# One constant product between every two heads of the first maxima, and batch 1's projections some heads later

## The chip, the cores and the metric

The kernel runs on one core of one Trainium2 chip, as one launch. The metric is the device time of one execution in microseconds. Before the change it was 619.75 us, the median of three runs (617.78 to 620.05). One execution was taken by the hardware profiler: 615.73 us, of which 614.0 us are the span of its trace. Five engines work at once and meet through semaphores: PE (TensorE, matmuls), DVE (VectorE), ACT (ScalarE), POOL (GpSimd) and SP (SyncE, which here only starts DMAs). TensorE is granted one of two clocks, 1.2 or 2.4 GHz, which the profile writes as 0.50 and 1.00.

## The reference

Two layers work on x of 16 batches x 256 rows x 128 columns. The first is attention with 16 heads of 8 columns each, the second a transformer block with a mixture of 8 experts. The change lies in the first. Cut to what matters:

```
x = x + layernorm(attn(layernorm(x)))           # layer 1
    qkv = x @ w_qkv.T + b_qkv                    # 16 heads of 8 columns
    a   = softmax(q @ k.T / sqrt(128))           # per batch and head: 256 x 256
    out = (a @ v) @ w_o.T + b_o + x
x = x + layernorm(ffn(layernorm(x)))            # layer 2
    y = layernorm(x + mha(x));  z = layernorm(y + moe(y))   # argmax over 8 experts
```

All of it is float32.

## The kernel before

Layer 1 computes the scores of every head twice. The first time (line 203, `scores_for_max`) the queries stand on the partitions, so that DVE can take each query's maximum over the keys straight from PSUM (line 357, `maxima`). The maxima are turned by DVE and written by SP's DMAs into a further row of the tile `q`. The second time (line 220, `scores`) the keys stand on the partitions, the maximum is subtracted as that further row, ACT takes the exponential (line 529), and PE multiplies with the values (line 234, `attend`).

A head has only 8 columns, and its operands lie in one of four strips of 32 partitions, `32 * (h % 4)`. A head's first scores use 24 of the array's 128 rows (or 8, for heads 12 to 15, whose keys are in `kraw`), its second scores 26 or 27. A head is two matmuls of 128 x 256 in float32, one for each half of the rows; the trace has two records for each of these, so four records for a head. The heads are issued in the order n = 0 to 15 with h = n ^ 2, so that consecutive heads lie in different strips.

PE's work is an order written out by hand. After the start (weights turned, batch 0 normalised and projected, seven constant products), a first stage makes the sixteen maxima of batch 0 and has nothing else of that batch to do. Batch 1's preparation is put between its heads: `prep_x(1)` turns the normalised x on PE (line 170), `prep_qk` makes queries and keys (line 177) and `prep_v` the values (line 185). Then come the iterations i = 0 to 16. Each has eight groups g, and in group g stand two heads of the first scores of batch i+1 and two heads of the second scores of batch i, now and then an attend (g = 3, 5, 7, and 1 for the last quarter of batch i-1), and the preparation of batch i+2.

PE waits in `scores_for_max` until DVE has read the PSUM bank of three heads before (`a_free`), and in `prep_x(1)` until POOL has normalised batch 1 (`xn_ok`, line 644). `keep_warm(n)` (line 161) is n matmuls of constant bfloat16 tiles, 128 x 128 by 128 x 512, into `psO`; nobody reads the result. The names in rows: `km` and `kraw` are keys, `qp` and `q` queries, `psA` the bank of the first scores, `psB` of the second, `psO` of the attends, `misc` of the preparation, `warm` the constant tile.

Layer 2 works on x when layer 1 has ended, at about 313 us.

Of the kernel before, what the change touches and what calls it, by code (L numbers as in the profile page):

```python
# [34 lines left out]
def first_layer(nc, x, w_qkv, b_qkv, w_o, b_o, ident, identh, minus_half, xs, out, kept, loads2, loaded2, w, loads,  # L35
                loaded):

    with ExitStack() as ctx:
# [66 lines left out]
        def fits(i, d):  # L105

            return 0 <= i + d <= LAST
# [46 lines left out]
        def _(pe):  # L154
            T = nc.tensor

            def begin(*name):

                pe.wait_ge(S["free"], turns[name])

            def keep_warm(n):

                for _ in range(n):
                    T.matmul(psO[:, :], warm[:, 0:P], warm[:, :], start=True, stop=True)

            def prep_x(b):
                begin("xT", b)
                pe.wait_ge(S["xn_ok"], b + 1)
                for c in range(2):
                    last = T.transpose(misc[:, c * P:(c + 1) * P], xn[:, b % 2, c, :], ident[:, :])  # L170
                last.then_inc(S["full"], 1)

            def prep_qk(b, k, t):
                if t == 0:
                    pe.wait_ge(S["free"], turns[("xT", b)] + 1)
                    begin("qk"[k], b)
                made = T.matmul(misc[:, t * L1:(t + 1) * L1], wqk[:, k, t, :], xnT[:, b % 2, :], start=True,  # L177
                                stop=True)
                if t == 1:
                    made.then_inc(S["full"], 1)  # L180
# [8 lines left out]
            def prep_v(b):  # L189
                begin("v", b)  # L190
                token_major(xnT[:, b % 2, :], 0)

            def scores_for_max(b, n):

                h = n ^ 2
                if n == 0:
                    pe.wait_ge(S["q_ok"], 4 * b + 4)
                    pe.wait_ge(S["k_ok"], 2 * b + 2)
                    pe.wait_ge(S["km_ok"], b + 1)
                pe.wait_ge(S["a_free"], count(16 * b + n - 2))  # L200
                depth = 24 if h < 12 else C1
                for c in range(2):
                    last = T.matmul(psA[:, (16 * b + n) % 3, c * L1:(c + 1) * L1],  # L203
                                    query_part(b, h, depth, c),
                                    keys(b, h, depth, slice(0, L1)), start=True, stop=True)
                last.then_inc(S["a_full"], 1)

            def scores(b, h):

                if h % HALF == 0:  # L210
                    pe.wait_ge(S[f"mrow{h // HALF}"], 16 * HALF * (b + 1))
                if b < LAST or h < 3:
                    pe.wait_ge(S["b_free"], count(16 * b + h - 2))
                elif h < 5:
                    pe.wait_ge(S["a_free"], 16 * B1)
                else:
                    pe.wait_ge(S["b_free"], 16 * b + h - 4)
                depth = 26 if h < HALF else 27
                for c in range(2):
                    last = T.matmul(bank_of(b, h)[:, c * L1:(c + 1) * L1],  # L220
                                    keys(b, h, depth, slice(c * P, (c + 1) * P)), queries(b, h, depth, slice(0, L1)),
                                    start=True, stop=True)
                last.then_inc(S["b_full"], 1)

            def attend(b, quad):

                pe.wait_ge(S["b_free"], 16 * b + 4 * quad + 4)
                if quad == 0:
                    pe.wait_ge(S["v_ok"], b + 1)
                if quad % 2 == 0:  # L230
                    pe.wait_ge(S["o_ev"], 2 * b + quad // 2)
                for c in range(2):
                    for j in range(4):
                        last = T.matmul(psO[32 * j:32 * j + 32, (quad % 2) * L1:(quad % 2 + 1) * L1],  # L234
                                        v32[:, b % SLOTS, c, 4 * quad + j, :], pr[:, (4 * quad + j) % PRING, c, :],
                                        start=(c == 0), stop=(c == 1))
                last.then_inc(S["av_done"], 1)

            def project(b):
                pe.wait_ge(S["onT_ok"], b + 1)  # L240
                begin("out", b)
                token_major(onT, 1)

            def iteration(i):
                here, next_, done = fits(i, 0), fits(i, 1), fits(i, -1)
                for g in range(8):
                    if next_:
                        scores_for_max(i + 1, 2 * g)
                        scores_for_max(i + 1, 2 * g + 1)
                    if here and next_:  # L250
                        scores(i, 2 * g)
                        scores(i, 2 * g + 1)
                    if here and not next_ and g % 2 == 0:
                        for h in range(2 * g, 2 * g + 4):
                            scores(i, h)
                    if here and g in (3, 5, 7):
                        attend(i, g // 2 - 1)
                    if g == 0 and i >= 2 and here:
                        prep_v(i)
                    if g == 1 and done:  # L260
                        attend(i - 1, 3)
                    if g == 1 and fits(i, 2):
                        prep_x(i + 2)
                    if g in (2, 4) and fits(i, 2):
                        prep_qk(i + 2, g // 2 - 1, 0)
                        prep_qk(i + 2, g // 2 - 1, 1)
                    if g == 6 and done:
                        project(i - 1)
# [35 lines left out]
            keep_warm(7)  # L304
            for n in range(16):
                scores_for_max(0, n)
                if n == 1:
                    prep_x(1)
                if n in (3, 5):
                    prep_qk(1, n // 2 - 1, 0)  # L310
                    prep_qk(1, n // 2 - 1, 1)
                if n == 7:
                    prep_v(1)
                if n in (9, 11, 13):
                    keep_warm(2)
            pe.wait_ge(S["v_ok"], 1)
            for i in range(LAST + 2):
                iteration(i)
# [1449 lines left out]
```

## Time and profile before

| | |
|---|---|
| runs, median (lowest to highest) | 619.75 us (617.78 to 620.05) |
| profiled execution | 615.73 us |
| its span | 614.0 us |
| mean granted clock of TensorE | 0.891 |
| PE busy, whole span | 522.8 us, 85% |
| DVE busy | 451.0 us, 73% |
| ACT busy | 359.4 us, 59% |
| POOL busy | 312.6 us, 51% |

The shares are over two layers with different limits, so they don't say what one stage waits for. The stage of the change runs from 12.55 us (head 0 of the first maxima) to 38.1 us, and iteration 0 from there to about 59.3 us. A matmul's time in the trace contains its way through the array, so the time that one step costs PE is read from start to start.

### The profile page before, as it was taken

To read this page: it belongs to the slowest core of one execution; us is meant where nothing else is said; L and a number is where in the kernel's file an instruction comes from. 1 tells how busy PE (TensorE), PEld (TensorE's weight loads), DVE (VectorE), ACT (ScalarE), POOL (GpSimd) and SP (SyncE) were. 2 spreads that over 40 slices of the span, in tenths; PEclk is the share of its full clock that TensorE was granted. 3 is DMA by queue.
4 is the path that set the end of the run, shared out by engine and by line. 5 is a ranking of instruction groups with operands and counts; after the bars stand their busy time and mean duration, and the time that the engine had idled before them with its cause. 6 is when DMAs were issued, how large, how long until landed. Compare 5 with 4: busy or idle time off the path is not lost. (4 is left out here: it accounts for less than half of the span.)

```text
span 614.0 us, 15928 instructions
## 1 busy us (share of the span) xinstructions
PE 522.8 (85%) x5194; PEld 375.8 (61%) x5194; DVE 451.0 (73%) x1278; ACT 359.4 (59%) x976; POOL 312.6 (51%) x522
## 2 busy tenths in 40 slices
PE   7999999999999999999954799988866269999910
PEld 4556666666666656666633577766645269999910
DVE  4346788888888879888833789999586626788860
ACT  3216667666776755676641798877643035776660
POOL 5402233344455546622234548878884600467776
PEclk9558999999999989999995999999856569999975
DMA  6001423111001110101120000000010222244233
GB/s 188 1 1 28 149 70 56 24 24 20 6 18 20 19 21 19 19 5 19 20 53 17 36 2 2 1 4 11 21 39 34 88 55 64 33 65 61 28 35 30
DMA packets 36036, 21.62 MB, mean 35 GB/s; under 512 B 11242, under 2 KB 34291, under 8 KB 35956
## 3 DMA queue, kind: packets, MB, share of 16 engines
q1 hardware_dynamic: 18450, 10.65, 7.5%
q0 software_dynamic: 6640, 4.92, 5.7%
q10 hardware_dynamic: 10866, 5.03, 3.1%
q8 instruction: 43, 0.70, 0.5%
q14 instruction: 37, 0.30, 0.2%
HBM read 10.11 MB, written 8.12 MB: 30 GB/s over the span
## 5 line engine op out<-in xcount | busy, mean ns | idle before, releaser
L357 DVE TENSOR_REDUCE nmax<-psA 128x2 f32<-128x512 f32 x256 | 164.8, 686 | 55.8 <-PE psA L203 55.1
L529 ACT ACTIVATE pr<-psB 128x512 f32<-128x512 f32 x250 | 136.0, 595 | 97.7 <-PE psB L220 96.4
L203 PE MATMUL psA<-km,qp 24*128 24x256 f32 x768 | 127.4, 426 | 1.4 <-DVE nmax L357 1.4
L220 PE MATMUL psB<-q,km 26*128 26x256 f32 (+1 forms) x752 | 112.0, 414 | 0.2 <-DMA q<-mT 0.2
L203 PEld LDWEIGHTS psA<-km,qp 24*128 24x128 f32 x768 | 79.5, 197 | 35.0 <-DVE nmax L357 24.0
L1689 POOL DMA_INDIRECT out<-wz,ys x39 | 63.3, 1624 | 53.3 <-ACT wz L1644 44.4
L657 POOL TENSOR_TENSOR km<-kraw,rows_of 128x768 f32<-128x768 f32 x15 | 22.0, 1467 | 113.4 <-ACT kraw L503 113.4
L220 PEld LDWEIGHTS psB<-q,km 26*128 26x128 f32 (+1 forms) x752 | 69.8, 191 | 1.4 <-DMA q<-mT 1.1
L234 PE MATMUL psO<-pr,v 128*32 128x256 f32 x1024 | 69.5, 389 | 0.1
L1241 ACT ACTIVATE prob<-psS,nbias 128x128 f32<-128x128 f32 x128 | 45.5, 384 | 8.6 <-DVE nbias L1059 8.5
L234 PEld LDWEIGHTS psO<-pr,v 128*32 128x32 f32 x1024 | 27.0, 110 | 33.1 <-issue 21.6
L1545 DVE TENSOR_TENSOR hT<-psH,e_nb1T 128x512 f32<-128x512 f32 x39 | 27.0, 692 | 25.8 <-PE psH L1506 17.8
L1506 PE MATMUL psH<-yT,own 128*128 128x128 f32 x312 | 42.7, 281 | 0.0
L203 PE MATMUL psA<-kraw,qp 8*128 8x256 f32 x256 | 41.3, 416 | 0.0
L1520 PE MATMUL psO<-e_w,hT 128*128 x312 | 41.2, 275 | 0.0
L1357 POOL DMA_INDIRECT y_sorted<-y_all,slot_i x32 | 32.4, 1012 | 16.9 <-DVE slot_i L1108 9.0
L1506 PEld LDWEIGHTS psH<-yT,own 128*128 128x128 f32 x312 | 39.5, 199 | 0.0
L1627 ACT ACTIVATE own<-e_w 128x512 f32 x39 | 24.3, 623 | 23.6 <-PEq L813 18.1
L1520 PEld LDWEIGHTS psO<-e_w,hT 128*128 128x128 f32 x312 | 38.0, 192 | 0.0
L177 PE MATMUL misc<-xnT,wqk 128*128 128x256 f32 x120 | 36.4, 429 | 0.2
L220 PE MATMUL psB<-q,kraw 27*128 27x256 f32 x248 | 36.0, 400 | 0.0
L630 POOL TENSOR_SCALAR ve<-mv_r 128x2 f32<-128x2 f32 x16 | 3.8, 236 | 61.3 <-DVE mv_r L331 61.3
(227 smaller groups left out, 1136.2 us busy)
## 6 DMA issues: line engine op xcount, KB each, us to landing
q<-mT SPq DMA_DIRECT2D x256, 1.0 KB
ys<-y_sorted SPq DMA_DIRECT2D x39, 72.0 KB, 1.9
e_w<-W ACTq DMA_DIRECT2D x1, 2048.0 KB
e_w<-W ACTq DMA_DIRECT2D x4, 512.0 KB
xs<-x_all SPq DMA_DIRECT2D x16, 128.0 KB
out<-x_all SPq DMA_DIRECT2D x15, 128.0 KB, 3.7
x_all<-x SPq DMA_DIRECT2D x1, 1536.0 KB, 10.3
out<-wz,ys POOLq DMA_INDIRECT x39, 3.3
```

The costliest lines, as they stand in the source:

```text
L177: made = T.matmul(misc[:, t * L1:(t + 1) * L1], wqk[:, k, t, :], xnT[:, b % 2, :], start=True, stop=True)
L203: last = T.matmul(psA[:, (16 * b + n) % 3, c * L1:(c + 1) * L1], query_part(b, h, depth, c), keys(b, h, depth, slice(0, L1)), start=True, ...
L220: last = T.matmul(bank_of(b, h)[:, c * L1:(c + 1) * L1], keys(b, h, depth, slice(c * P, (c + 1) * P)), queries(b, h, depth, slice(0, L1)), ...
L234: last = T.matmul(psO[32 * j:32 * j + 32, (quad % 2) * L1:(quad % 2 + 1) * L1], v32[:, b % SLOTS, c, 4 * quad + j, :], pr[:, (4 * quad + j ...
L357: V.tensor_reduce(nmax[:, b % 2, hf, :, at], psA[:, (16 * b + n) % 3, :].rearrange("p (c m) -> p c m", c=2), AX.X, ALU.max, negate=True).t ...
L529: A.activation(pr[:, h % PRING, :, :].rearrange("p c l -> p (c l)"), bank_of(b, h), ACT.Exp, scale=SCALE1).then_inc(S["b_free"], 1)
L1241: A.activation(prob[:, n, c, h, :], psS[s][:, u * P:(u + 1) * P], ACT.Exp, bias=nbias[:, s, u:u + 1], scale=SCALE2, accum_out=den[:, n, c, ...
L1357: G.indirect_dma_start(y_sorted, bass.IndirectOffsetOnAxis(slot_i[:, j:j + 1], 0), y_all[:, j, :], None).then_inc(sent, 16)
L1506: last = T.matmul(psH[t % 2][:, f * P:(f + 1) * P], own[:, t % 3, f * P:(f + 1) * P], yT[:, t % 3, :], start=True, stop=True)
L1520: last = T.matmul(to, hT[:, t % 2, f, :], w["w2"][:, f, bass.ds(e, P)], start=False, stop=(f == NF - 1))
L1545: V.tensor_tensor(hT[:, t % 2, :, :], psH[t % 2][:, :].rearrange("p (f n) -> p f n", f=NF), w["nb1T"][:, bass.ds(e, NF)].unsqueeze(2).broa ...
L1689: G.indirect_dma_start(out, bass.IndirectOffsetOnAxis(ids[:, t % RING, P:P + 1], 0), wz[:, t % WRING, :], None, compute_op=ALU.add).then_i ...
```

## The change

Before, the constant products of the first stage came in three groups of two, after n = 9, 11 and 13, and batch 1's preparation after n = 1 (x), 3 and 5 (queries, keys) and 7 (values). Heads 0 and 1, 2 and 3 and so on stood side by side.

After, the preparation comes after n = 4, 6, 8 and 10, three constant products after n = 2, and one after each of the eleven other heads. Iteration 0 gets two constant products in each of its groups 0 and 1. In all there are fourteen constant products in the first stage in place of six, and four in iteration 0 in place of none. The computation is the same.

```diff
@@ iteration(i) of PE
                     if here and g in (3, 5, 7):
                         attend(i, g // 2 - 1)
+                    if i == 0 and g in (0, 1):
+                        keep_warm(2)
                     if g == 0 and i >= 2 and here:
                         prep_v(i)
@@ the first stage of PE
             keep_warm(7)
             for n in range(16):
                 scores_for_max(0, n)
-                if n == 1:
+                if n == 2:
+                    keep_warm(3)
+                elif n == 4:
                     prep_x(1)
-                if n in (3, 5):
-                    prep_qk(1, n // 2 - 1, 0)
-                    prep_qk(1, n // 2 - 1, 1)
-                if n == 7:
+                elif n in (6, 8):
+                    prep_qk(1, n // 2 - 3, 0)
+                    prep_qk(1, n // 2 - 3, 1)
+                elif n == 10:
                     prep_v(1)
-                if n in (9, 11, 13):
-                    keep_warm(2)
+                else:
+                    keep_warm(1)
             pe.wait_ge(S["v_ok"], 1)
             for i in range(LAST + 2):
                 iteration(i)
```

The first place is PE's stream at the start of the first maxima. A row is a matmul as issued; `x4` of line 203 is two heads side by side, `x2` is one head. Before:

```order
L164 MATMUL psO<-warm 128x512 x7
L203 MATMUL psA<-km,qp 128x256 x4
L170 MATMUL misc<-ident,xn 128x128 x2
L203 MATMUL psA<-km,qp 128x256 x4
L177 MATMUL misc<-xnT,wqk 128x256 x2
L203 MATMUL psA<-km,qp 128x256 x4
L177 MATMUL misc<-xnT,wqk 128x256 x2
```

The same place after the change:

```order
L164 MATMUL psO<-warm 128x512 x7
L203 MATMUL psA<-km,qp 128x256 x2
L164 MATMUL psO<-warm 128x512
L203 MATMUL psA<-km,qp 128x256 x2
L164 MATMUL psO<-warm 128x512
L203 MATMUL psA<-km,qp 128x256 x2
L164 MATMUL psO<-warm 128x512 x3
L203 MATMUL psA<-km,qp 128x256 x2
L164 MATMUL psO<-warm 128x512
L203 MATMUL psA<-km,qp 128x256 x2
L170 MATMUL misc<-ident,xn 128x128 x2
```

No two heads stand side by side any more, here or in the rest of the stage: there is a constant product or a piece of preparation between any two.

The second place is PE's stream from the last heads of the stage into iteration 0, where a group of the iteration is a row of line 203 and one of line 220. Before:

```order
L203 MATMUL psA<-kraw,qp 128x256 x4
L203 MATMUL psA<-km,qp 128x256 x4
L220 MATMUL psB<-q,km 128x256 x4
L203 MATMUL psA<-km,qp 128x256 x4
L220 MATMUL psB<-q,km 128x256 x4
L170 MATMUL misc<-ident,xn 128x128 x2
```

The same place after the change:

```order
L203 MATMUL psA<-kraw,qp 128x256 x2
L164 MATMUL psO<-warm 128x512
L203 MATMUL psA<-km,qp 128x256 x4
L220 MATMUL psB<-q,km 128x256 x4
L164 MATMUL psO<-warm 128x512 x2
L203 MATMUL psA<-km,qp 128x256 x4
L220 MATMUL psB<-q,km 128x256 x4
L164 MATMUL psO<-warm 128x512 x2
L170 MATMUL misc<-ident,xn 128x128 x2
```

The groups of iteration 0 keep their heads side by side; two constant products come behind each of the first two. The other engines' streams have the same instructions in the same order as before.

## Rows read from the trace of the kernel before

**Rows 1.** The page's 40 slices: PE busy and granted clock in tenths.

```profile
PE   7999999999999999999954799988866269999910
PEclk9558999999999989999995999999856569999975
```

**Rows 2.** Stretches: length, busy us (instructions) of PE, PEld, DVE, ACT, POOL, clock, DMA.

```profile
10.00:16.00 6.00, 4.43 (x29) 2.73 (x29) 4.51 (x15) 2.13 (x6) 2.91 (x7) 1.00 0.56 154
16.20:22.00 5.80, 5.80 (x20) 3.42 (x17) 2.08 (x4) 0.84 (x2) 0.29 (x1) 0.50 0.01 3
...
28.00:35.20 7.20, 7.20 (x24) 2.79 (x22) 3.42 (x6) 0.00 (x0) 3.78 (x9) 0.50 0.01 1
...
43.00:50.20 7.20, 7.20 (x47) 4.29 (x50) 2.62 (x8) 2.39 (x5) 0.00 (x0) 0.50 0.02 3
50.40:59.30 8.90, 8.90 (x116) 5.50 (x108) 6.94 (x14) 6.83 (x16) 4.24 (x7) 1.00 0.01 3
60.00:200.00 140.00, 139.46 (x1704) 88.42 (x1696) 119.76 (x273) 96.06 (x202) 59.34 (x101) 1.00 0.19 45
```

**Rows 3.** Who waited for whom from 60 to 300 us: total, times, longest.

```profile
DVE nmax L357 <- PE psA L203: 32.9, 71, 2.0
```

**Rows 4.** PE in order of time around the fall: start, us, operation, records, idle before.

```profile
10.95 1.67 PE L164 MATMUL psO<-warm 128*128 128x512 bf16 x7
12.55 1.14 PE L203 MATMUL psA<-km,qp 24*128 24x256 f32 x8
15.26 0.41 PE L170 MATMUL misc<-ident,xn 128*128 128x128 f32 x2 [1.57 <-POOL xn L644]
15.60 1.57 PE L203 MATMUL psA<-km,qp 24*128 24x256 f32 x8
```

**Rows 5.** PE in order of time: a pair and two constant products, later a lone head.

```profile
26.29 2.08 PE L203 MATMUL psA<-km,qp 24*128 24x256 f32 x8
28.31 1.03 PE L164 MATMUL psO<-warm 128*128 128x512 bf16 x2
29.27 2.08 PE L203 MATMUL psA<-km,qp 24*128 24x256 f32 x8
...
35.80 0.76 PE L203 MATMUL psA<-km,qp 24*128 24x256 f32 x1
...
36.35 0.63 PE L203 MATMUL psA<-km,qp 24*128 24x256 f32 x1
...
36.78 1.05 PE L203 MATMUL psA<-km,qp 24*128 24x256 f32 x2
```

**Rows 6.** PE in order of time in iteration 10, a head alone at full clock.

```profile
214.16 1.13 PE L203 MATMUL psA<-km,qp 24*128 24x256 f32 x4
215.67 0.48 PE L203 MATMUL psA<-km,qp 24*128 24x256 f32 x1 [0.39 <-DVE nmax L357]
...
216.85 0.71 PE L185 MATMUL misc<-wvo,xnT 128*128 128x128 f32 x4
```

**Rows 7.** Stretches around the same place, columns as in Rows 2.

```profile
210.00:217.40 7.40, 7.01 (x78) 4.66 (x72) 7.15 (x12) 4.09 (x9) 6.96 (x9) 1.00 0.02 3
217.60:220.90 3.30, 3.30 (x32) 1.90 (x32) 2.33 (x8) 1.76 (x4) 2.38 (x6) 0.50 0.02 4
```

**Rows 8.** PE in order of time in iteration 0: first group, rise of the clock, end.

```profile
38.09 0.79 PE L203 MATMUL psA<-km,qp 24*128 24x256 f32 x1 [0.25 <-DVE nmax L357]
...
49.69 1.35 PE L234 MATMUL psO<-pr,v 128*32 128x256 f32 x16
50.97 0.49 PE L203 MATMUL psA<-km,qp 24*128 24x256 f32 x2
...
52.06 1.13 PE L177 MATMUL misc<-xnT,wqk 128*128 128x256 f32 x4
...
59.22 0.49 PE L203 MATMUL psA<-km,qp 24*128 24x256 f32 x2
```

**Rows 9.** The page's costliest group: DVE's maxima.

```profile
L357 DVE TENSOR_REDUCE nmax<-psA 128x2 f32<-128x512 f32 x256 | 164.8, 686 | 55.8 <-PE psA L203 55.1
```

## The prediction

> **What bounds the kernel now.** I read the 40 slices first. PE is busy nine tenths or more nearly everywhere in the first half, and in slices 1 and 2 its clock is at 0.5 although PE is full [rows 1]. So the stretches of time come next. From 16.2 to 50.2 us the granted clock is 0.50, the lower of the two levels, and PE is busy without a gap: 7.20 of 7.20 us in two of the stretches [rows 2]. From 50.4 us on it is 1.00, and stays so over the 140 us that follow. The waits show that DVE waits for PE's scores 71 times between 60 and 300 us, 32.9 us in all [rows 3]: in layer 1 PE is what the others wait for, and time that PE loses or wins early in the layer arrives at its end. Layer 2's work on x can't start before that, so it arrives at the end of the kernel too.
>
> The order of time shows what the clock did at its fall. PE worked through seven constant products and two heads, then waited 1.57 us for POOL's normalised x, turned it, and was in the middle of the next two heads when the clock fell at about 16.2 us [rows 4]. It rose at about 50.3 us, while the first attend of iteration 0 was running, with a projection and the two heads of each kind shortly before it [rows 8]. What the change can win is therefore the wait (1.57 us) and a part of the 34 us at the lower clock. What it costs is read from start to start of PE's steps.
>
> **What a step costs.** At the lower clock two heads side by side take 26.29 to 28.31, 2.02 us, for eight records [rows 5]. The two heads lie in different strips of the array and run at the same time. A lone head is seen in the same stage: its four records start at 35.80, 36.35 and (two) from 36.78 on, with a busy time of 1.05 from 36.78, so it ends at 37.83, 2.03 us after its start; at first the pair before it still ran in other strips, its last records ran alone [rows 5]. A head alone costs what two heads cost. At the full clock the same holds: eight records 1.14 us [rows 4], four records of a lone head 1.13 us [rows 6]; from start to start a full-clock block is 50.97 to 52.06, 1.09 us [rows 8]. I take 1.07, and 2.02/1.07 = 1.89 as the ratio between the two clocks.
>
> The page "TensorE: Matmul & The Clock Gate" of the Trainium skill says in "Part 3: Packing small matmuls" that matmuls in different row strips run concurrently and that matmuls stay in order. It speaks against this change: a full-height product between two heads takes the partner away from each. The trace has the same thing with its own numbers, above.
>
> Seven constant products take 10.95 to 12.55, 1.60 us, or 0.23 each at the full clock [rows 4], so 0.43 each at the lower one by the ratio. Two of them there take 28.31 to 29.27, 0.96 us, change of operation included [rows 5]. A single one between two heads isn't in the trace at either clock. Its bounds are 0.43 (no more than its stream) and 0.96 (as much as two); I take 0.96 - 0.43 = 0.53, since the pair's row is the nearest.
>
> **The sum, on the path of the clock as it was.** All of it lies on PE, which is the engine waited for.
> - Lost pairs: eight blocks of two heads become sixteen of one. 8 x 2.02 = +16.2 us.
> - Constant products of the first stage: before 3 x 0.96 = 2.9; after eleven single ones, 5.8, and one group of three, 0.96 + 0.43 = 1.4, so 7.2. +4.3 us (bounds: +3.2 to +9.1).
> - Iteration 0: two groups of two, +1.9 us (+1.0 if the clock is full there). Its heads stay side by side.
> - The wait: -1.6 us. Batch 1's x was ready at 15.2 us, and `prep_x(1)` now comes after five heads, so it waits for nothing. Queries, keys and values of batch 1 come later by some heads, but are wanted only in iteration 0 and after it. DVE needs 0.69 us for a head's maxima [rows 9] against 2.5 us of PE, so it waits more and delays nobody; the PSUM bank is always free.
> - The full-clock time before the fall, from 12.55 to 16.2, is now full of work. The 1.57 us that were a wait do work that would cost 1.57 x 1.89 = 2.97 later: -1.4 us beyond the wait itself.
>
> This gives +19.4 us. Moved preparation costs the same wherever it stands.
>
> **The clock's own path.** Two terms are left. The fall can come somewhat later than 16.2, since the gap before it is filled. What the trace shows for lone heads at the full clock is iteration 10: a lone head for 1.13 us, 0.39 us of waiting, three heads at once, a small projection, and then the clock is at 0.50 for 3.3 us, where PE had been busy 7.01 of the 7.40 us before [rows 6, 7]. The new stage is a row of such lone heads with products between. And from 28.0 to 35.2 three blocks of two heads alternated with three groups of two products, 100% busy, and the clock stayed at 0.50 [rows 2]; the new stage has fewer products per microsecond (0.53 in 2.55 us of a step, before 0.96 in 2.98). So it should fall early and not rise again inside the stage. I allow 0 to 6 us more at full clock and take 2; each is worth 0.89: -1.8 us. The rise in iteration 0 came 12.2 us after the iteration began at 38.1 [rows 8]. With four products in its first groups it can come earlier, 0 to 9 us; I take 5, each worth 1 - 1/1.89 = 0.47: -2.4 us.
>
> 19.4 - 1.8 - 2.4 = +15.2 us. The profiled execution was 615.7 (614.0 of span, 1.7 around it), 4.0 below the median of the runs; on the profile's own footing I expect 630.9, and against the median of 619.75 it is 635. Bounds of this case: with 6 and 9 us both at their best +9.9, with both at zero +19.4, and with the single product at 0.43 or 0.70 another -1 or +2. Own range 628 to 641.
>
> **Rivals.**
> - The clock holds. "Part 1: The HAM clock gate" of the page named above, in the Trainium skill, ties the clock to how busy PE has been, and a reader of that alone would expect a filled PE to keep it; the trace disagrees by the 34 us of full PE at 0.50 [rows 2]. As a mechanism here: the only gap in front of the fall goes, and PE stays at 1.00 from 12.55 on. The old stage at full clock would be 2.1 (the old full part without the wait) + 21.65/1.89 = 13.6 us; the eight lost pairs add 8 x 1.07 = 8.6, eight more products 8 x 0.23 = 1.8: 24.0 against 25.5. Iteration 0 turns 12.1 us into 6.4 and adds 0.9: -4.8. In all -6.3: 613.5. Since a microsecond at the lower clock costs 0.47, this rival decides up to some 13 us at the lower clock between 12.55 us and the old rise; with more the kernel is slower. Against it stands iteration 10 [rows 6, 7].
> - A return in the middle: the clock falls early, and the two projections with full array after n = 6 and 8 bring it back at about n = 8. Before, the first of them stood in the stretch from 16.2 to 22.0 us with two heads on each side, and the clock stayed at 0.50 [rows 2]. By the ratio: about 14.2 of 24.0 full-clock us lie before that point, 3.65 of them run full, so (14.2 - 3.65) x 0.89 = 9.4 us are lost: 24.0 + 9.4 = 33.4 against 25.5, +7.9, and iteration 0 gives -4.8. +3.1: 623.
> - The pairs are not lost: a head overlaps with something else in the array, and only products and wait count: 4.3 + 1.9 - 1.6 - 1.4 - 2.4 = +0.8: 620.5. Against it stand both lone heads [rows 5, 6]; constant products never overlapped with the heads beside them.
> - It falls and iteration 0 stays at the lower clock until its end at 59.2 [rows 8]: +19.4 and (59.2 - 50.3) x 0.89 = 7.9, 647. The attend that stood before the old rise is still there, so this is unlikely.
>
> **Chances.** The forecast 0.74; the clock holds 0.09; a return in the middle 0.08; pairs not lost 0.05; low through iteration 0 0.04. A difference under 0.5%, 3 us, can't be told from no change. Faster by more than that is the first rival, 0.09. The third rival and the margin of the second give 0.04 for no change. The rest, 0.87, is slower. The range reaches from the return in the middle to the top of the forecast's own: 622 to 641.
>
> **What the profile after would show.** The rows of line 164 with one product at a time between `x4` rows of line 203, each head some 2.0 us from its start to the product; clock 0.50 from somewhere in 16 to 22 us to about 60; the start of iteration 0 (the first row of line 220) at about 53 instead of 38; the wait of line 170 gone; L357's waits for PE longer in the first stage. After iteration 0 the same picture as before, some 15 us later. I would be wrong if the clock is at 1.00 in the stage, or if a head followed by a product takes less than 1.8 us at the lower clock.

## The result, and the profile after

The changed kernel took 632.09 us in the median of four runs (624.35 to 637.01) against 619.75 us (617.78 to 620.05). The ratio is 1.0226, with a 95% interval from 1.0154 to 1.0297 (the two medians alone give 1.020): slower, as forecast (635, 622 to 641). That it is slower is clear of the noise; whether by more than 2% is not. The profiled execution is the quickest of the four, 624.35 us with a span of 622.6, so 8.6 us above the profiled one of before.

The page of the kernel after: PE's busy share and the granted clock in 40 slices of 15.6 us, and DVE's maxima with their idle time. The answers to [rows 1] and [rows 9].

```profile
PE   8999999999999999999963899999857259999910
PEclk9658899999999999999995999797766569999975
...
L361 DVE TENSOR_REDUCE nmax<-psA 128x2 f32<-128x512 f32 x256 | 165.5, 686 | 62.1 <-PE psA L203 61.3
```

The clock holds into slice 1 and is low in slice 2 and the beginning of slice 3. DVE's maxima (L361 here is line 357 of the kernel before) cost the same and wait 6 us longer for PE. The stretches of the same kernel, columns as in [rows 2]:

```profile
12.30:21.50 9.20, 8.95 (x35) 5.20 (x36) 5.01 (x12) 0.39 (x2) 3.40 (x7) 1.00 0.13 31
21.70:49.30 27.60, 27.13 (x56) 14.55 (x56) 7.38 (x15) 2.78 (x7) 7.20 (x14) 0.50 0.00 1
49.40:52.20 2.80, 2.47 (x18) 1.39 (x18) 1.17 (x4) 0.54 (x2) 0.00 (x0) 0.50 0.01 4
52.40:65.80 13.40, 13.38 (x157) 8.71 (x156) 9.97 (x22) 9.23 (x20) 3.66 (x7) 1.00 0.02 3
66.10:69.30 3.20, 3.20 (x32) 1.89 (x25) 1.11 (x3) 0.98 (x2) 0.29 (x1) 0.50 0.58 154
```

The clock is 1.00 to 21.6 us, 0.50 to 52.3, and once more 0.50 from 66.0 to 69.4. PE in order of time, the answer to [rows 4, 5 and 8]: start, busy us, operation, records, idle before.

```profile
12.26 1.13 PE L203 MATMUL psA<-km,qp 24*128 24x256 f32 x4
13.64 1.13 PE L203 MATMUL psA<-km,qp 24*128 24x256 f32 x4 [0.25 <-issue]
14.69 0.39 PE L164 MATMUL psO<-warm 128*128 128x512 bf16 x1
15.01 1.13 PE L203 MATMUL psA<-km,qp 24*128 24x256 f32 x4
...
19.26 0.44 PE L170 MATMUL misc<-ident,xn 128*128 128x128 f32 x2
...
24.45 2.07 PE L203 MATMUL psA<-km,qp 24*128 24x256 f32 x4
26.45 0.61 PE L164 MATMUL psO<-warm 128*128 128x512 bf16 x1
26.98 2.07 PE L203 MATMUL psA<-km,qp 24*128 24x256 f32 x4
...
49.38 0.80 PE L203 MATMUL psA<-km,qp 24*128 24x256 f32 x2
...
65.86 1.44 PE L234 MATMUL psO<-pr,v 128*32 128x256 f32 x12
```

Each row of line 203 is now one head (`x4`, before `x8` for two), and one head takes 24.45 to 26.45, 2.00 us, at the lower clock. A product between two heads takes 26.45 to 26.98, 0.53 us. (The record of one product at 13.3 us is missing from the trace; its time is there as "issue".) The wait in front of line 170 is gone. Who waited from 12 to 50 us:

```profile
DVE nmax L361 <- PE psA L203: 24.5, 16, 3.3
```

Each of the sixteen maxima waits for PE, which is full. Before, from 12 to 38.1 us, these waits came to 13.9 us.

| from start to start | before | after | |
|---|---|---|---|
| first maxima (first head to iteration 0) | 12.55 to 38.09: 25.5 us | 12.26 to 49.38: 37.1 us | +11.6 |
| iteration 0 to its last attend | 38.09 to 58.22: 20.1 us | 49.38 to 65.86: 16.5 us | -3.6 |
| the rest | to 614.0 | to 622.6 | +1.0 |

(The stage began 0.3 us earlier in the profile after, which makes up the total of 8.6, but for rounding.)

The boundary at 38.09 is not a clean one. The rows from 35.80 on in [rows 5] are no head of the stage: they are the first head of iteration 0, which began beside the stage's last pair. Of that pair these rows are the beginning:

```profile
35.23 0.80 PE L203 MATMUL psA<-kraw,qp 8*128 8x256 f32 x2
35.82 1.07 PE L203 MATMUL psA<-kraw,qp 8*128 8x256 f32 x4
```

By the price of a pair it ended at about 37.25 (35.23 + 2.02, an estimate); the second head of iteration 0 waited for DVE and started at 38.09. So some 0.84 us of the 25.5 belong to iteration 0. In the profile after, both first heads of iteration 0 start at 49.38, and there is no such piece.

### The profile page after: what moved, and what is told of

It reads as the page before. It is cut to its first block and busy times, and to the rows that moved or that the text cites. A ratio compares the mean times of both kernels' runs of the same rounds, so it can differ in the third digit from the quotient of the medians.

```text
span 622.6 us, 15949 instructions
## 1 busy us (share of the span) xinstructions
PE 534.8 (86%) x5203; PEld 383.9 (62%) x5206; DVE 449.5 (72%) x1278; ACT 358.7 (58%) x976; POOL 314.1 (50%) x522
## 5 line engine op out<-in xcount | busy, mean ns | idle before, releaser
L361 DVE TENSOR_REDUCE nmax<-psA 128x2 f32<-128x512 f32 x256 | 165.5, 686 | 62.1 <-PE psA L203 61.3
L203 PE MATMUL psA<-km,qp 24*128 24x256 f32 x768 | 130.2, 413 | 1.9 <-DVE nmax L361 1.1
L220 PE MATMUL psB<-q,km 26*128 26x256 f32 (+1 forms) x752 | 108.4, 405 | 0.0
L203 PEld LDWEIGHTS psA<-km,qp 24*128 24x128 f32 x768 | 80.9, 190 | 37.0 <-DVE nmax L361 22.2
L220 PEld LDWEIGHTS psB<-q,km 26*128 26x128 f32 (+1 forms) x752 | 67.5, 187 | 0.5 <-DMA q<-mT 0.4
L203 PE MATMUL psA<-kraw,qp 8*128 8x256 f32 x256 | 45.5, 417 | 0.0
L1361 POOL DMA_INDIRECT y_sorted<-y_all,slot_i x32 | 32.6, 1019 | 16.9 <-DVE slot_i L1112 9.0
L1631 ACT ACTIVATE own<-e_w 128x512 f32 x39 | 24.3, 624 | 23.8 <-PEq L817 18.2
L203 PEld LDWEIGHTS psA<-kraw,qp 8*128 8x128 f32 x256 | 29.2, 192 | 10.8 <-DVE nmax L361 6.5
L177 PE MATMUL misc<-xnT,wqk 128*128 128x256 f32 x120 | 35.4, 420 | 0.3
```

Source lines behind the costliest of these rows:

```text
L220: last = T.matmul(bank_of(b, h)[:, c * L1:(c + 1) * L1], keys(b, h, depth, slice(c * P, (c + 1) * P)), queries(b, h, depth, slice(0, L1)), ...
L361: V.tensor_reduce(nmax[:, b % 2, hf, :, at], psA[:, (16 * b + n) % 3, :].rearrange("p (c m) -> p c m", c=2), AX.X, ALU.max, negate=True).t ...
L1361: G.indirect_dma_start(y_sorted, bass.IndirectOffsetOnAxis(slot_i[:, j:j + 1], 0), y_all[:, j, :], None).then_inc(sent, 16)
```

## The experiments

Theory L: the loss is the pairs. A full-height product or a piece of preparation between any two heads makes sixteen blocks of eight. Rival P: the loss is the twelve more constant products. Rival C: the moved preparation lets the clock fall. Each ratio below is to the kernel before on the same chip, whose median was 619.78 us beside e1 to e4 and 617.88 beside e5 to e8; it stands with its 95% interval and differs from the quotient of the medians by up to 0.4%. The changed kernel did not run beside them, so where a run is compared with its 632.09 us the ratios are the better guide. All stages named in the text are read in the one profiled execution of each kernel. The line numbers in rows move by up to four with each edit: L207 and L181 of e2_strip are L203 and L177 before, and L356 of e5_late_prep is L357.

**Heads in pairs again (e1_pairs).** All fourteen products of the changed kernel and its preparation, one head later still, behind odd heads alone (`...` stands for calls of the preparation, here and below):

```diff
-                if n == 2:
-                    keep_warm(3)
-                elif n == 4:
+                if n == 5:
                     prep_x(1)
-                elif n in (6, 8):
+                if n in (7, 9):
                     ...
-                elif n == 10:
+                if n == 11:
                     prep_v(1)
-                else:
-                    keep_warm(1)
+                keep_warm({1: 2, 3: 4, 5: 1, 7: 1, 9: 1, 11: 1, 13: 2, 15: 2}.get(n, 0))
```

> The changed kernel with its heads in pairs again: all fourteen constant products and the same late preparation, but only behind a head of odd number, so that two heads stand side by side (products after n = 1, 3, 5, 7, 9, 11, 13, 15: 2, 4, 1, 1, 1, 1, 2, 2). Theory L (the lost pairs are the price): eight blocks fewer, 8 x 2.0 = 16 us at the lower clock, so 616 or less; since work is then packed closer the clock may also hold, and the first maxima then end near 28 us and not 49: 605 to 612. Rival P (the twelve more constant products are the price): they are all still there, so 628 to 634. Rival C (the moved preparation lets the clock fall and that is the price): also 628 to 634.

Measured: 608.91 us, ratio 0.9818 (0.9749 to 0.9887). Same work as the changed kernel, and by the medians 23 us faster (the ratios are 0.9818 and 1.0226). Its stretches and first rows:

```profile
12.70:28.30 15.60, 15.60 (x91) 9.40 (x92) 11.03 (x25) 3.17 (x8) 7.17 (x14) 1.00 0.08 19
28.50:31.70 3.20, 3.20 (x19) 1.41 (x18) 1.66 (x5) 0.58 (x2) 2.86 (x8) 0.50 0.02 3
31.90:45.30 13.40, 13.38 (x157) 8.65 (x156) 9.98 (x22) 9.23 (x20) 3.87 (x8) 1.00 0.02 3
```

```profile
12.61 1.14 PE L203 MATMUL psA<-km,qp 24*128 24x256 f32 x8
13.69 0.60 PE L164 MATMUL psO<-warm 128*128 128x512 bf16 x2
```

The stage ends at 28.85 us, after 16.2 us, at full clock to its last pair. That is 20.9 us less than the changed stage, and not the pairs alone: the changed stage's work, put to the full clock, is 9.4 + 27.8/1.89 = 24.1 us, so the pairs are 7.9 of the 20.9 and the clock, which now holds, is 13.0. P and C have no place left as the main cost: the products and the late preparation are both there.

**Pairs lost without any product (e2_strip).** The kernel before, with heads that share a strip side by side in batch 0's first maxima:

```diff
+        def first_order(n):
+            return n // 8 * 8 + n % 8 // 2 + 4 * (n % 2)
-                h = n ^ 2
+                h = first_order(n) if b == 0 else n ^ 2
```

> The kernel before, with one difference: in batch 0's first maxima the heads come in the order 0 4 1 5 2 6 3 7 8 12 9 13 10 14 11 15, so that the two heads side by side share a strip of the array and cannot run at the same time. No product is added and nothing else moves. Theory L: a pair takes eight records one after the other, at the lower clock 8 x 0.43 + 0.3 = 3.7 us in place of 2.0, so 8 x 1.7 = +14 us: 630 to 636. Rivals P and C: nothing that they name is changed, so 618 to 621.

Measured: 630.83 us, ratio 1.0175 (1.0118 to 1.0232). Some 11 of the changed kernel's 12 us, with no product added. Two heads in PE's order of time, and the stretches:

```profile
15.34 3.77 PE L207 MATMUL psA<-km,qp 24*128 24x256 f32 x8
19.05 2.07 PE L181 MATMUL misc<-xnT,wqk 128*128 128x256 f32 x4
```

```profile
15.10:49.20 34.10, 34.10 (x80) 21.71 (x79) 9.80 (x18) 3.17 (x8) 8.19 (x16) 0.50 0.01 2
49.30:62.70 13.40, 13.40 (x88) 8.44 (x85) 6.87 (x15) 5.53 (x11) 0.00 (x0) 0.50 0.01 2
```

The two heads take 3.71 us, as worked out, against 2.02 side by side in different strips. The stage lasts from 12.15 to 49.2 us, 37 us, as long as the changed one. This run isolates the pairs, since its clock takes nearly the old course: it falls at 15.0 us (before 16.2) and rises 13.5 us into iteration 0 (before 12.2).

**The products of iteration 0 alone (e3_it0).**

```diff
+                    if i == 0 and g in (0, 1):
+                        keep_warm(2)
```

> The kernel before with only the change's four constant products in groups 0 and 1 of iteration 0. Cost 1.9 us at the lower clock; the rise of the clock may come earlier by up to 9 us, each worth 0.47. Theory L: between +2 and -2.5 us, 617 to 622. Rival P (a constant product costs far more than its stream, about 1 us each over the whole path): +4, 624.

Measured: 614.98 us, ratio 0.9944 (0.9879 to 1.0009), so the sign isn't certain; it is below the expected 617 to 622. The stretches of its trace:

```profile
15.40:38.20 22.80, 22.55 (x79) 12.46 (x79) 9.29 (x19) 3.10 (x8) 7.92 (x16) 0.50 0.01 1
38.40:45.90 7.50, 7.50 (x46) 4.34 (x50) 3.72 (x10) 2.55 (x5) 0.00 (x0) 0.50 0.01 2
46.10:56.80 10.70, 10.68 (x128) 6.74 (x120) 7.71 (x15) 7.49 (x16) 3.63 (x7) 1.00 0.02 4
```

The clock rises 7.8 us after the iteration's start in place of 12.2, and the time from that start to the last attend falls from 20.1 to 18.7 us. This part of the change costs nothing here and may give a little.

**The stage alone (e4_noit0).** The changed kernel without the two lines of e3_it0.

```diff
-                    if i == 0 and g in (0, 1):
-                        keep_warm(2)
```

> The changed kernel without its four constant products in iteration 0; the first stage is the changed one. Theory L: the stage holds the whole loss, so as slow as the changed kernel: 629 to 636, later rise of the clock in iteration 0 than 3 us after its start. Rival P: a third of the added products gone, so a third of the loss: 628.

Measured: 636.43 us (635.98 to 636.83), ratio 1.0276 (1.0226 to 1.0326), 0.4 us above the expected 629 to 636. Its stretches:

```profile
13.00:16.80 3.80, 3.80 (x15) 2.17 (x16) 2.17 (x7) 0.00 (x0) 3.37 (x7) 1.00 0.25 60
17.00:54.60 37.60, 37.60 (x78) 19.73 (x76) 10.05 (x19) 3.16 (x8) 7.21 (x14) 0.50 0.00 1
54.70:68.00 13.30, 13.30 (x86) 8.48 (x86) 6.46 (x15) 5.02 (x11) 0.00 (x0) 0.50 0.01 2
```

Here the clock fell at 16.9 us, although the stage is word for word that of the changed kernel, whose clock fell at 21.6. The stage lasts 12.90 to 54.62, 41.7 us against 37.1 there. Counted from each stage's own start, the full clock lasted 4.0 us here and 9.4 there: 5.4 us at 0.89 each are 4.8, where 4.6 was measured. So the moment of the fall differs between executions of the same instructions, and with it this stage is 11.6 or 16.2 us longer than before. The clock rose 13.5 us after the iteration's start, against 3 us with the products, and iteration 0 took 20.8 us to its last attend, against 16.5.

**The late preparation alone (e5_late_prep).**

```diff
-                if n == 1:
+                if n == 5:
                     prep_x(1)
-                if n in (3, 5):
+                if n in (7, 9):
                     ...
-                if n == 7:
+                if n == 11:
                     prep_v(1)
```

> The kernel before with only batch 1's preparation moved: x, queries, keys and values of batch 1 behind n = 5, 7, 9 and 11 in place of 1, 3, 5 and 7; the six constant products stay behind 9, 11 and 13, heads in pairs. The first wait of 1.6 us goes. Theory L: the move costs nothing, 616 to 620, with the clock falling near 16 us as before. Rival W (the wait is what lets the clock fall, so without it the clock holds through the stage): 603 to 608.

Measured: 610.85 us, ratio 0.9851 (0.9783 to 0.9918), between the two theories and better than L said. In its trace the wait for POOL is gone and the clock falls all the same:

```profile
12.34 1.15 PE L203 MATMUL psA<-km,qp 24*128 24x256 f32 x12
14.32 3.18 PE L203 MATMUL psA<-km,qp 24*128 24x256 f32 x12 [0.83 <-DVE nmax L356]
17.43 0.69 PE L170 MATMUL misc<-ident,xn 128*128 128x128 f32 x2
```

```profile
12.40:15.50 3.10, 2.27 (x20) 1.74 (x20) 2.73 (x9) 0.00 (x0) 2.63 (x6) 1.00 0.44 107
15.70:36.80 21.10, 20.63 (x70) 11.65 (x69) 8.57 (x18) 3.17 (x8) 7.77 (x15) 0.50 0.01 1
```

With nothing between the first six heads PE now waits 0.83 us for DVE instead. But this profiled execution is the slowest of the four (617.66; the others 608.4 to 612.6), so it doesn't show where the others gained. It refutes rival W only as a certainty: the wait for POOL is not needed for the fall. What the wait does in the other executions stays open. With the heads in pairs the late preparation is no cost: the whole interval lies below 1. Why the median is 7 us lower, when the wait was 1.6, isn't shown.

**Pairs, with products where the heads are thin (e6_dense), and the same with iteration 0's products (e8_dense_it0).** The preparation stands as in e5_late_prep, and thirteen products replace the six, eight of them behind the last three pairs, two of which have heads of 8 rows. e8_dense_it0 has the lines of e3_it0 besides.

```diff
+                keep_warm({1: 2, 3: 2, 5: 1, 11: 2, 13: 3, 15: 3}.get(n, 0))
```

> Heads in pairs, preparation behind n = 5, 7, 9, 11, and twelve... in all thirteen constant products, more of them where a pair has only 8 rows: behind n = 1, 3, 5, 11, 13, 15: 2, 2, 1, 2, 3, 3; none in iteration 0. Theory L with the clock: the stage runs at full clock to its end (in the run with pairs the clock fell at 28.4 us, behind the pairs of 8 rows), 602 to 608. Rival P (products cost more than they give): above the 609 of the run with pairs.

> The kernel of e6_dense with the change's four constant products in iteration 0 as well. If the clock is at 1.00 when iteration 0 begins, they cost 4 x 0.22 + 0.2 = 1.1 us and give nothing: 1 us above e6_dense. If it had fallen there, they bring it back earlier: up to 3 us below.

Measured: 604.31 us, ratio 0.9752 (0.9683 to 0.9821), and 603.74 us, ratio 0.9764 (0.9700 to 0.9827). The stretches of e6_dense:

```profile
12.30:28.00 15.70, 15.49 (x92) 9.29 (x95) 11.52 (x27) 3.16 (x9) 7.83 (x15) 1.00 0.11 28
28.10:43.20 15.10, 15.08 (x170) 10.18 (x168) 11.54 (x25) 10.02 (x21) 6.46 (x13) 1.00 0.02 4
43.30:200.00 156.70, 155.96 (x1905) 98.61 (x1906) 133.96 (x301) 107.78 (x226) 68.21 (x111) 1.00 0.19 42
```

From 12.3 to 200 us the lower clock doesn't come at all: stage 15.6 us (12.26 to 27.89), the maxima of DVE (16 x 0.69 = 11.0) now fairly close behind, iteration 0 15.3 us. Both kernels beat the one before by some 14 us and, by the medians, the changed one by some 28. The four products in iteration 0 make no difference that can be measured; what they were forecast to cost there, 1.1 us, is smaller than the intervals. In the trace of e8_dense_it0 iteration 0 takes 15.4 us, and PE waits 0.6 us in it for the DMA that writes the maxima into `q` (0.2 in e6_dense): with PE at full clock throughout, something else begins to hold it up.

**Lone heads kept at full clock (e7_lone_three).** The changed kernel's lone heads with three products behind each but n = 6 and 8, and none in iteration 0:

```diff
-                if n == 2:
-                    keep_warm(3)
-                elif n == 4:
+                if n == 4:
                     ...
-                else:
-                    keep_warm(1)
+                if n not in (6, 8):
+                    keep_warm(3)
```

> The changed kernel's lone heads and preparation, but three constant products behind each head but n = 6 and 8 (42 in all), none in iteration 0. It separates the two parts of the loss. Theory L: the clock holds at 1.00 and a lone head then costs 1.07 us, so 16 x 1.07 + 42 x 0.22 + preparation 3.0 + changes 1.2 = 30.6 us for the stage against 25.5, and iteration 0 gains 4 to 6: 617 to 623, faster than the changed kernel in spite of 28 more products. Rival: if lone heads let the clock fall whatever stands between, 42 products at 0.43 and sixteen blocks of 2.0 take some 60 us: 650.

Measured: 623.59 us (615.1 to 627.1), ratio 1.0114 (1.0032 to 1.0197): 0.6 us above the expected 617 to 623, and far from the rival's 650.

```profile
16.20:46.50 30.30, 29.82 (x118) 15.65 (x120) 12.66 (x27) 3.19 (x9) 10.60 (x21) 1.00 0.00 1
46.60:61.80 15.20, 15.20 (x170) 10.34 (x170) 11.10 (x24) 9.97 (x21) 3.63 (x7) 1.00 0.02 4
```

```profile
19.78 1.13 PE L203 MATMUL psA<-km,qp 24*128 24x256 f32 x4
20.84 0.82 PE L164 MATMUL psO<-warm 128*128 128x512 bf16 x3
21.59 1.13 PE L203 MATMUL psA<-km,qp 24*128 24x256 f32 x4
```

The stage lasts 16.16 to 46.53, 30.4 us, where 30.6 was worked out, at 1.00 throughout. With 28 products more in it the stage is 6.7 us shorter than the changed one, since it has the clock. The medians agree (623.59 against 632.09), though the two intervals of the ratio overlap a little; and the mean granted clock of all ten runs is 0.898 to 0.914, of the changed kernel's four 0.872 to 0.882.

It is 19 us slower than e6_dense. Of that the two traces show 14.7 us in the stage: eight lost pairs at 1.06 (8.5) and 29 more products at 0.22 (6.4) make 14.9. The profiled execution also began the stage 3.9 us later than that of e6_dense. No instruction before that point was changed, but eight of them, batch 0's projections of queries and keys, took 3.63 us where e6_dense has 1.96: the step of the lower clock (read from the rows; the windows give 1.00 there). So the price of the pairs is there at either clock, and nearly double at the lower (2.02 against 1.06).

## Why the prediction was right

**The lost pairs** were put at eight blocks of 2.02. A lone head took 2.00 us in the profile after, two heads in one strip 3.71 (e2_strip), which alone made the kernel before 11 us slower. Putting the pairs back (e1_pairs) turned 632.09 into 608.91, but there the clock changed as well. Shown, and the main term. The row from which the prediction read the price of a lone head was the first head of iteration 0 and not one of the stage; the price holds all the same.

**The single product**, not in the trace before and taken at 0.53 between 0.43 and 0.96, was 0.53.

**The wait** went, as said. **The moved preparation** cost nothing, as said (e5_late_prep); what it gained in the runs was not foreseen.

**The fall of the clock** was allowed 0 to 6 us later and taken at 2. From the stage's start on, the full clock lasted 3.63 us before, 9.36 in the profiled execution after and 3.99 in that of e4_noit0, with the same instructions: 5.73 and 0.36 later. Put into the sum, 16.2 + 4.3 - 1.6 - 1.4 = 17.5, and 17.5 - 5.73 x 0.89 = +12.4 us for the stage against +11.6 measured; with 0.36 it is +17.2 against +16.2. The step was right, the size is one that the executions spread over. The 0.8 and 1.0 us that are left over are about the size of a term that the prediction had at nothing: the 0.84 us by which 38.09 lies behind the stage's last pair. That piece is gone in the profile after, and the prediction took 38.1 for the plain start of iteration 0.

**The rise in iteration 0** was taken at 5 us earlier; it was 9.2 in the profile after and 4.4 in e3_it0. For the iteration that gives +1.0 (the four products counted at the full clock, since the time at the lower one is counted by itself) and -9.2 x 0.47 = -4.3, so -3.3, against -3.6; in e3_it0 +1.0 - 2.1 = -1.1, against -1.4. This term was undersized for the profiled execution.

**The total**, +15.2, is an execution with a fall at 18.2 us and a rise 7 us into the iteration. The profiled one had both better and is 8.6 us above, so 6.6 below the 630.9 that were expected on its footing, and iteration 0 began at 49.4 and not at about 53; the median of the runs is 12.3 above. That the median came so near to 15.2 rests on a choice inside a spread: 2 and 5 us were picked from 0 to 6 and 0 to 9. The runs carry their mean granted clock: 0.882 at 624.35 us and 0.872 at 633.01. The time at the lower clock is twice one minus that, by the span: 146.9 us of 622.6 and 161.6 us of 631.3, 14.7 us more, which at 0.47 cost 6.9 of the 8.7 between the two. At 631.17 us (0.875) it is 4.9 of 6.8, but at 637.01 (0.876) only 5.0 of 12.7, so there most of the difference is not the clock and stays open. That it was this stage that had the lower clock in those runs is argued, not shown: only one execution has a trace.

**The rivals.** The clock didn't hold. It did hold with the products behind pairs (e1_pairs to 28.4 us, e6_dense to the end of the stage and beyond), and with lone heads too where three products stood behind nearly each (e7_lone_three). So neither the lone heads nor the filled gap decide it alone, and what does is not shown. A return in the middle was not seen in either trace of this stage. The pairs were lost. Iteration 0 did not stay low.

## What to carry to other kernels

Here work in one strip of the array was free beside work in another: at the lower clock one head took 2.00 us and two in different strips 2.02, and in e5_late_prep the first three heads side by side took 1.15 us at the full clock, where one alone took 1.13. A product of full height between two heads took that away. So put such products behind a set of heads in different strips, not inside it. Read the price of a constant product from the block that it cuts, not from its own 0.22 us at the full clock or 0.43 at the lower. And a clock that is to be held has to be checked in the trace: here fourteen products, one behind most lone heads, didn't hold it, with 42 it held, and behind pairs thirteen were enough.

## What the runs showed that I had not expected

The same stage, instruction for instruction, kept the full clock until 21.6 us in one execution and until 16.9 in another (after, e4_noit0), and the kernel before ranged from 608.25 to 623.72 us in thirteen runs. A change of one per cent in such a kernel is not told from one profile.

With lone heads and three products each the clock stayed at 1.00 through 30 us in which PE had no two heads side by side; with one product each it fell, with PE equally full: 8.95 of 9.20 us in front of the fall and 27.13 of 27.60 behind it, against 29.82 of 30.30.
